# Narrow tiles of row maxima packed two to a PSUM bank, in a causal attention kernel with 20 units of maxima per head pair in place of 26

## What is computed

```python
x = x + 0.5 * ffn(layernorm(x))
x = x + attention(layernorm(x))      # 16 heads of 64, rotary embedding, causal
x = x + 0.5 * ffn(layernorm(x))

scores = einsum('bhid,bhjd->bhij', q, k) * 64 ** -0.5
probs = softmax(where(causal, scores, -inf))
out = einsum('bhij,bhjd->bhid', probs, v)
```

## Time and profile before

| | |
|---|---|
| median of 3 runs | 1354.47 us (1351.78 to 1355.27) |
| the profiled execution | 1352.74 us, its span 1351.0 us |
| TensorE (PE) busy | 1287.3 us, 95% |
| VectorE (DVE) busy | 871.9 us, 65% |
| GpSimd (POOL) busy | 752.1 us, 56% |
| ScalarE (ACT) busy | 618.4 us, 46% |
| first feed-forward layer and set-up | to about 120 us |
| attention | about 120 to 1250 us |
| last feed-forward layer | about 1250 to 1351 us |
| mean granted TensorE clock | 0.977 of full speed |

### The profile page before, as it was taken

The page is one execution under the profiler, slowest core; times in us unless marked ns, Lnnn a source line. Parts: engine busy times, 40 slices in busy tenths (PEclk is TensorE's granted clock), DMA queues, the critical chain, the costliest instruction groups (busy, mean ns, idle before and its releaser), DMA issues. The chain is left out here.

```text
span 1351.0 us, 24951 instructions
## 1 busy us (share of the span) xinstructions
PE 1287.3 (95%) x6240; PEld 735.7 (54%) x6240; DVE 871.9 (65%) x2270; ACT 618.4 (46%) x1176; POOL 752.1 (56%) x454
## 2 busy tenths in 40 slices
PE   5987599999999999999999999999999999999798
PEld 2544355555555555556555656555555555555365
DVE  5566556677676767676767676767676767664254
ACT  3664134444444444444444444444444444444474
POOL 4134155666565656566666666666666666665300
PEclk9998679999999999999999999999999999999799
DMA  7022546565555556464646464646464646452001
GB/s 275 38 93 87 143 118 159 119 157 121 146 130 131 145 120 156 111 163 113 157 115 161 105 161 108 162 107 162 107 162 105 162 108 162 107 119 52 0 24 39
DMA packets 113612, 165.86 MB, mean 123 GB/s; under 512 B 13360, under 2 KB 63408, under 8 KB 113456
## 3 DMA queue, kind: packets, MB, share of 16 engines
q1 hardware_dynamic: 112784, 163.96, 47.6%
q10 hardware_dynamic: 800, 1.57, 0.6%
HBM read 37.29 MB, written 10.49 MB: 35 GB/s over the span
## 5 line engine op out<-in xcount | busy, mean ns | idle before, releaser
L916 POOL TENSOR_TENSOR psum_p<-psum_p,shared_a 128x256 f32<-128x256 f32 (+1 forms) x192 | 280.8, 1462 | 93.2 <-ACT shared_a L718 83.7
L718 ACT ACTIVATE shared_a<-bank 128x512 f32<-128x512 f32 (+3 forms) x512 | 201.5, 445 | 253.3 <-PE bank L577 251.1
L560 PE MATMUL bank<-k_hh,q_hl 128*128 128x512 f32 (+3 forms) x768 | 258.0, 390 | 15.9 <-DMA k_hh<-parts 10.1
L577 PE MATMUL bank<-q_hm,k_l 65*128 65x512 f32 (+3 forms) x768 | 244.7, 373 | 0.0
L799 DVE TENSOR_REDUCE max_left<-bank 128x1 f32<-128x512 f32 x256 | 175.7, 688 | 101.1 <-PE bank L560 100.9
L560 PEld LDWEIGHTS bank<-k_hh,q_hl 128*128 128x128 f32 x768 | 138.3, 193 | 179.0 <-issue 78.0
L571 PE MATMUL bank<-q_hl,k_hh 128*128 128x512 f32 (+3 forms) x768 | 227.6, 350 | 1.9 <-ACT shared_a L718 1.7
L718 ACT ACTIVATE probs_more<-bank 128x512 f32<-128x512 f32 (+1 forms) x256 | 132.2, 568 | 193.0 <-PE bank L577 175.3
L803 DVE CUSTOM_DVE_ANT_0 max_scratch<-bank,tri_mask,max_left 128x128 f32<-128x128 f32 (+3 forms) x256 | 138.0, 548 | 110.6 <-PE bank L560 110.6
L597 PE MATMUL bank<-shared_a,v_cur 128*64 128x512 f32 (+3 forms) x1024 | 203.0, 475 | 0.0
L894 POOL TENSOR_TENSOR parts<-rotated,parts 128x1024 fp32r<-128x1024 f32 x64 | 152.5, 2383 | 48.4 <-ACT parts L693 48.4
(11 more groups left out here) (127 smaller groups left out, 1916.5 us busy)
## 6 DMA issues: line engine op xcount, KB each, us to landing
q_hl<-parts SPq DMA_DIRECT2D x252, 128.0 KB, 2.8
k_hh<-parts SPq DMA_DIRECT2D x252, 128.0 KB, 2.7
xn_cur<-xn_scratch SPq DMA_DIRECT2D x16, 1024.0 KB, 6.7
v_cur<-shared_b SPq DMA_DIRECT2D x32, 512.0 KB, 6.0
k_l<-parts SPq DMA_DIRECT2D x63, 256.0 KB, 5.2
q_hm<-parts SPq DMA_DIRECT2D x63, 256.0 KB, 5.2
w_qk<-w_scratch SPq DMA_DIRECT2D x32, 256.0 KB, 3.1
w_scratch<-first_w_parts SPq DMA_DIRECT2D x8, 512.0 KB, 3.1
```

The lines of the kernel that those rows point to most:

```text
L560: nc.tensor.matmul(max_bank[k % 2][:, 0:w], q_hl[u][h][:, q * P:(q + 1) * P], k_hh[u][h][:, keys * CHUNK:keys * CHUNK + w], start=True, st ...
L577: nc.tensor.matmul(scores[h][:, x0:], k_l1[u][h][:, keys], q_hm[u][h][:, q], start=False, stop=True).then_inc(scores_full, 1)
L718: nc.scalar.activation(probs_of(s)[:, h, x0:], scores[h][:, x0:], ACT.Exp, scale=SCORE_SCALE).then_inc(probs_done, 1)
L916: last = nc.gpsimd.tensor_tensor(acc, acc, new, ALU.add)
```

## The change

The tiles of 128, 256 and 384 keys are put side by side into one bank, two to a unit: 128 with 384 columns, or 256 with 256. A unit may now hold a list of tiles. TensorE waits once per unit and signals with its last matmul; VectorE waits once, reduces the tiles one after the other and signals with the last. The 512-wide tiles remain units of their own. There are 20 units per pair instead of 26, the transposes being units 5 and 19, and they are laid out anew over the steps. The matmuls, their sizes and the reductions are the same ones.

```diff
+        def diagonal(c, *tiles):
+            x0 = list(itertools.accumulate((P * (q % 4 + 1) for _, q in tiles), initial=0))
+            return [(c, h, q, c, x) for (h, q), x in zip(tiles, x0)]
+
+        def left(h, q):
+            return [(1, h, q, 0, 0)]
+
-        MAX_UNITS = ([(0, h, i, 0) for h in range(2) for i in range(4)] + [(0, None, None, None)] +
-                     [(1, h, i + b, k) for h in range(2) for i in (4, 6) for k in range(2) for b in range(2)] + [(1, None, None, None)])
+        MAX_UNITS = [diagonal(0, (0, 0), (0, 2)), diagonal(0, (1, 0), (1, 2)), diagonal(0, (0, 1), (1, 1)), diagonal(0, (0, 3)),
+                     diagonal(0, (1, 3)), [],
+                     left(0, 4), left(0, 6), left(0, 5), diagonal(1, (0, 4), (0, 6)), left(1, 4), left(1, 6), left(1, 5),
+                     diagonal(1, (1, 4), (1, 6)), left(0, 7), diagonal(1, (0, 5), (1, 5)), left(1, 7), diagonal(1, (0, 7)),
+                     diagonal(1, (1, 7)), []]
         NT = len(MAX_UNITS)
-        ROWS_UNIT = [8, NT - 1]
-        MAX_AHEAD = {4: (2, 3), 5: (6, 7), 6: (8, 9), 7: (11,), 8: (13,), 10: (18,), 11: (20, 21)}
-        MAX_BEHIND = {3: (0, 1), 4: (4, 5), 6: (10,), 7: (12,), 8: (14, 15), 9: (16, 17), 10: (19,), 11: (22,)}
-        MAX_LATE = (23, 24)
+        ROWS_UNIT = [5, NT - 1]
+        MAX_AHEAD = {4: (1,), 5: (3,), 6: (5, 6), 7: (8,), 8: (10,), 10: (14,), 11: (16,)}
+        MAX_BEHIND = {3: (0,), 4: (2,), 5: (4,), 6: (7,), 7: (9,), 8: (11,), 9: (12, 13), 10: (15,), 11: (17,)}
+        MAX_LATE = (18,)
...
-        EARLY_MAX = range(9, 15)
-        FIRST_MAX = {0: range(15, 18), 1: range(18, 21), 2: range(21, 24), 3: range(24, 26)}
+        EARLY_MAX = range(6, 10)
+        FIRST_MAX = {0: range(10, 13), 1: range(13, 15), 2: range(15, 17), 3: range(17, 20)}
...
-                    w = CHUNK if keys < c else P * (q % 4 + 1)
-                    nc.tensor.matmul(max_bank[k % 2][:, 0:w], q_hl[u][h][:, q * P:(q + 1) * P],
-                                     k_hh[u][h][:, keys * CHUNK:keys * CHUNK + w], start=True, stop=True).then_inc(max_full, 1)
+                    for _, h, q, keys, x0 in MAX_UNITS[k]:
+                        w = CHUNK if keys < c else P * (q % 4 + 1)
+                        last = nc.tensor.matmul(max_bank[k % 2][:, x0:x0 + w], q_hl[u][h][:, q * P:(q + 1) * P],
+                                                k_hh[u][h][:, keys * CHUNK:keys * CHUNK + w], start=True, stop=True)
+                    last.then_inc(max_full, 1)
...
             def max_of(p, k):
-                c, h, q, keys = MAX_UNITS[k]
                 dve.wait_ge(max_full, NT * p + k + 1)
-                col = slice(4 * h + q % 4, 4 * h + q % 4 + 1)
-                if keys < c:
-                    nc.vector.reduce_max(max_left[:, col], max_bank[k % 2][:], AX.X).then_inc(max_free, 1)
-                else:
-                    w = P * (q % 4 + 1)
-                    settle(dve)
...
+                for c, h, q, keys, x0 in MAX_UNITS[k]:
+                    col = slice(4 * h + q % 4, 4 * h + q % 4 + 1)
+                    if keys < c:
+                        last = nc.vector.reduce_max(max_left[:, col], max_bank[k % 2][:], AX.X)
+                    else:
+                        w = P * (q % 4 + 1)
+                        settle(dve)
+                        last = nc.vector.tensor_tensor_reduce(
+                            out=max_scratch[k % 2][:, x0:x0 + w], in0=max_bank[k % 2][:, x0:x0 + w], in1=tri_mask[:, CHUNK - w:],
+                            scale=1.0, scalar=max_left[:, col] if c else -3e38, op0=ALU.add, op1=ALU.max,
+                            accum_out=max_all[c][:, col])
+                last.then_inc(max_free, 1)
```

More of the change, by code:

```diff
@@ L1 @@
+import itertools
 import concourse.bass as bass
@@ L549, in max_unit @@
             def max_unit(p, i, u, k):
-                c, h, q, keys = MAX_UNITS[k]
+                c = 0 if k <= ROWS_UNIT[0] else 1
                 if k in (0, ROWS_UNIT[0] + 1):
```

## The result

The changed kernel takes 1364.51 us (median of 4 runs, 1359.64 to 1366.29), the kernel before in the same comparison 1354.75 (1351.78 to 1355.27): a ratio of 1.0071, 95% interval 1.0041 to 1.0101. On another chip the unaltered change took 1361.38 against 1353.82, ratio 1.0062 (1.0045 to 1.0079). It is slower by 0.6 to 0.7%, and 1364.4 had been forecast.

A forecast was written before the change was run, and what follows sets the result against it. TensorE's matmul stream alone was taken to bound the steady state. Transpose wait 12.2 plus narrow tiles 0.7 less first pair 3.0 gave +9.9 us, 1364.4 us against the 1354.47 median; range 1353 to 1372.

The forecast's parts named there:

- The removed waits are worth nothing: Steady state, TensorE and VectorE: six waits and six signals fewer per pair save 0 us.
- Rival D: Loader's idle time is a stall shared equally by 26 waits: removing six saves 16 us, 1336 us; chance 0.08.
- The late transpose: Step 6, first rows' transpose: waits for unit 4's reduction behind add_to_x, 0.40 us a pair taken, 12.2 us together.
- the lower bound: Transpose's wait if add_to_x (L826) were out of the way: release at 2.30 us, wait 0.18 us.
- Rival B: The wait at the transpose is hidden after all: 1352.2 us, no measurable difference; chance 0.12.
- TensorE has none in which to make the time good: Behind the waiting transpose: ScalarE and GpSimd have slack, TensorE none, so the 0.40 us a pair is paid in full.
- Narrow tiles: 128-wide tiles ahead of another fp32r matmul hold 0.05 us extra; one more such: 0.7 us taken, 0 to 1.4.
- Unit 14's bank: One score step after units 12 and 13: some 0.1 us to spare for its bank, costed at 0.
- Two pairs 69.7 us: Sign in the steady stretch: two pairs take 69.7 us where they took 68.9.
- The first pair: Pair 0: fewer units ahead and step 2's 2.41 us wait gone; 3.0 us saved, bounds 0 and 4.
- about 1 us earlier: Sign in pair 0: first scores start about 1 us sooner, with four units made ahead of the pair, not six.
- Rival C: VectorE's operations do not overlap, each starting at the previous one's end: transpose waits 0.64 us, 1371.7 us; chance 0.10.

The follow-up runs named there:

- the move alone: Kernel before, 26 units, one 512-wide unit moved from ahead of step 5's product with V to behind it, nothing packed: 1361.38 us, ratio 1.006.
- unit 4 ahead: Changed kernel, everything packed, with unit 4 put back ahead of step 5's product with V: 1350.68 us, ratio 0.9972 to the kernel before.
- The last kernel: Packed kernel with unit 4 back ahead in step 5; unit 13 turned round and put ahead of step 10's product with V: 1349.85 us, ratio 0.9973.
- the five packed kernels: Changed kernel 1364.51 us; with add_to_x behind unit 4's reduction 1355.45; with unit 4 ahead 1350.68, also wide tiles first 1350.14, or narrow tile last 1349.85.

## Why the prediction was right

**The removed waits are worth nothing: nearly.** The transposes aside, the loader still idles for 52.5 us, and a steady pair with all tiles packed and the transpose in time (34.407 to 34.442) is no shorter than before (34.405). Rival D, which took the idle time of the earlier trace rows for stalls, falls with that. But the prediction looked for stalls by the idle time in the matmuls' rows alone, and so missed a wait for a bank that the kernel before does pay, once in two pairs, in step 10 of a pair without projections of V:

```profile
993.41 0.08 DVE L803 DVE_READ_ACCUMULATOR2_ANT max_all<- 128x1 f32 x1
...
993.55 0.19 PEld L560 LDWEIGHTS bank<-k_hh,q_hl 128*128 128x128 f32 x1 [0.17 <-DVE max_all L803]
...
993.55 0.50 PE L560 MATMUL bank<-k_hh,q_hl 128*128 128x512 f32 x1
993.98 0.65 PE L597 MATMUL bank<-shared_a,v_cur 128*64 128x256 f32 x4
```

The load comes 0.14 behind the reduction that frees the bank, as in the earlier trace rows, and together with its matmul. In the same place after it is hidden, 0.17 ahead:

```profile
998.65 0.19 PEld L573 LDWEIGHTS bank<-k_hh,q_hl 128*128 128x128 f32 x1
...
998.82 0.40 PE L573 MATMUL bank<-k_hh,q_hl 128*128 128x512 f32 x1
999.15 0.65 PE L611 MATMUL bank<-shared_a,v_cur 128*64 128x256 f32 x4
```

From the tile to the product it is 0.33 in place of 0.43, and the tile itself comes 0.17 in place of 0.19 behind the matmul ahead of it: 0.12 over two pairs, 0.06 a pair or 1.7 us in all, which the change gives back. It is not the stall at the transpose that does this: with the move alone, which has the stall, the distance is 0.43 still, and with unit 4 ahead, which has none, it is 0.33. Whether the packing by itself or the place of the units does it was not tested.

**The late transpose: right, in place, cause and size.** Forecast was a release 2.51 us after the start of unit 3; it is 2.50 (984.51 to 987.01). TensorE could have gone at 2.12 forecast, 2.12 by the trace (986.52 and 0.11). So the wait is 0.38 where 0.39 was worked out and 0.40 taken. In the pairs of the other parity it is 0.1 more, 0.48 to 0.49. The chain by which it came, unit 4 full, add_to_x in front of it, 0.14 from the accumulator read to the load, is the one of the trace, and the lower bound (2.30 without the addition) was met by a run of its own. Rival B, a wait hidden after all, was wrong by all of it.

**"TensorE has none in which to make the time good": nearly.** Summed over two pairs, one of each parity, the distances at the transpose grow by 0.86 and behind it by 0.08 (0.10 in place of 0.05 from the transpose to the next matmul). The bank wait of step 10 takes 0.12 off, and the narrow tiles add 0.12 (next paragraph). The sum is 0.94, and two pairs grew by 0.89 (mean of the stretch) to 0.91 (the two in the middle); the rest is spread over distances that differ by 0.01 to 0.02. So nearly nothing of the stall is made good.

**Narrow tiles, at most 0.05 a pair, 0.7 us taken: right in kind, at the upper bound in size.** Over two pairs all eight of them hold about 0.05 us more than their columns and the switch, 0.43 together, where six of the eight did so before, 0.31 together: 0.06 a pair, 1.8 us in all. The last kernel, with one of them ahead of a product again, has 0.33.

**Unit 14's bank, costed at 0: right**, no wait stands there. **Two pairs 69.7 us** were forecast, by the trace they take 35.52 + 34.18 = 69.7. Steady state in all: 12.9 us forecast (12.2 + 0.7), 29 x 0.446 + 0.3 for the last pairs = 13.2 measured. Of these last, pair 30 grew by 0.69 (0.6 forecast), and the last pair became 0.41 shorter, which was not forecast. That the sum comes so near is in part luck. At the transpose and behind it a pair loses 0.47 (half of 0.86 + 0.08) where 0.40 was taken, some 2 us in all, and the narrow tiles cost 1.1 us more than taken; the bank wait, put at nothing, gives 1.7 us back.

**The first pair, 3.0 us saved (0 to 4): right in mechanism, a little low in size.** TensorE in pair 0 after, from step 2 to 4:

```profile
163.88 1.08 PE L611 MATMUL bank<-shared_a,v_cur 128*64 128x512 f32 x4
...
166.41 0.39 PE L542 MATMUL bank<-xn_cur,w_qk 128*128 128x256 f32 x1 [1.45 <-DVE rotated L805]
...
170.48 0.48 PE L567 MATMUL bank<-ident,max_all 128*128 128x128 f32 x1 [2.16 <-DVE max_all L817]
```

The 2.41 us ahead of a maxima matmul are gone, and what is late next is the projection of step 2, as forecast, with 1.45 us; it was not forecast that the transpose would wait 2.16 us. From the scores of step 2 to those of step 3 it takes 4.44 us, before 6.96. With the tiles apart in the same steps it is 7.34, so here the packing itself does it: the third unit of a step no longer needs the first one's bank. From step 0 to step 4 it is 18.95 against 22.40. But this stage runs in part at TensorE's lower clock of 1.2 GHz, for 31 us here and 41 before between 138 and 210 us by the granted clock, and 31 to 41 in other runs without a rule by kernel; the 3.5 us of one profile are therefore not all the change's. By the rests of the table the five packed kernels and the repetition give 3.2 to 5.1 us, 4.4 in the mean. The one sign that failed is the first scores' "about 1 us earlier", for which 1.0 us had been put on the fewer units ahead: they start 0.10 earlier here (155.92 for 156.02), and from 1.9 earlier to 1.5 later in the other packed kernels. Where the rest beyond 3.0 comes from isn't settled.

**The sum**, +9.9 by the forecast, was 9.8 us on one chip and 7.6 on the other: 29 times the difference of the steady pairs is 12.9 and 12.6, less the rests of 3.2 and 5.1, where 3.0 had been taken.

**Rival C**, VectorE's operations end to end, falls: L817 at 985.04, L841 at 985.66, L817 at 986.26 and L798 at 986.87 are 0.62, 0.60 and 0.61 apart with durations of 0.69, 0.69 and 0.68. The wait would have been 0.64. The Trainium skill (VectorE: DVE Perf Modes, "The DRAIN you can't avoid") has the next operation start only when the pipe of the one before is empty, and adds that an operation which is not held starts earlier. The prediction named only the first half. In this trace each of these operations starts some 0.08 us before the end that the profile gives the one before.

## What to carry to other kernels

An idle weight loader is no stall until a matmul's start is late, and a late start need not carry an idle mark: compare distances from start to start in two places with unlike releasers before pricing a wait. When units of work are laid out anew, write down for each barrier, here a transpose that needs all tiles of its half, which unit is its last, and what stands between that unit and the barrier on every engine's queue; a wait of 0.4 us once per pair cost three times what the whole change earned, and one entry of a list gave it back. Packing small tiles into a bank pays where three would stand in a row on two banks, and little where the order already gives each bank time.

## What the runs showed that was not expected

- The idle mark of a late matmul understates the loss. The transpose's row says 0.22, from start to start 0.38 are lost there and 0.05 behind it; the windows show 6.98 us without a matmul where the stretch grew by 11.58. The matmul in front of it is shown as running for longer than it holds the engine.
- The same 512-wide tile, unit 3, reaches its reduction 0.53 us after its start in one parity and 0.64 in the other (1017.85 to 1018.49), with VectorE idle both times. This is the 0.1 by which the wait differs between the two; its cause stays open.
- A bank that comes free a little late costs time without any idle mark on a matmul: 0.12 us once in two pairs in the kernel before (993.55), 0.08 in each pair with unit 4 ahead (974.04). The sign is a weight load that starts 0.14 behind a reduction and no longer well ahead of its matmul.
- Putting the 128-wide tile ahead of the output projection hides nothing of its 0.05, ahead of a product with V all of it. Both the projection and the product are fp32; the output projection loads 128 columns of weights (128*128 in its rows), the product 64 at a time (128*64). That this is the difference was not tested by itself.
- Packing is worth 0.67 us a pair (tiles apart with unit 4 ahead) to 1.18 (tiles apart in the changed order) in the new layout, more than the few tenths expected, because single bank waits of up to 0.72 us appear where three units follow one another.
